# A graph layer with an expert mixture: six row buffers in the edge stage, two chunks of the first layer kept on chip

## The reference, cut to what matters

```python
# x [10000, 512]; src, dst [5000]; edge_attr [5000, 64]; dst is sorted
def gnn(x, edge_attr, edge_index, W_e, b_e, W1, b1, g1, beta1, W2, b2, g2, beta2, eps):
    src, dst = (edge_index[0], edge_index[1])
    msg = jax.nn.relu(x[src] + edge_attr @ W_e + b_e)
    aggr = jax.ops.segment_sum(msg, dst, num_segments=x.shape[0])
    h = (1.0 + eps) * x + aggr
    h = jax.nn.silu(_bn(h @ W1 + b1, g1, beta1))      # W1 [512, 1024]
    h = h @ W2 + b2                                   # W2 [1024, 512]
    return jax.nn.silu(_bn(h, g2, beta2))

x = x + gnn(_layernorm(x, axis=-1), ...)
x = x + ffn(_layernorm(x, axis=-1)[None], controller, f1, f2)[0]   # mixture of 16 experts
```

## Time and profile before

| | |
|---|---|
| median of 3 runs | 1946.03 (1945.61 to 1946.71) |
| profiled execution, its own time | 1943.54 |
| its span | 1941.8, mean granted clock 0.974 |
| TensorE busy | 1814.2, 93% |
| VectorE, ScalarE, GpSimd busy | 1184.6, 988.8, 364.1 |
| device memory | 171.31 MB read, 137.46 MB written |

### The profile page before, as it was taken

One profiled execution on the slowest core, in us unless ns is written; L12 is line 12 of the kernel. 1 busy time (PEld: TensorE's weight loads), 2 busy tenths in 40 slices (PEclk: granted clock), 3 DMA queues, 4 the chain that ended last, 5 costly groups with the idle time before them and its releaser, 6 DMA issues. The chain is left out here.

```text
span 1941.8 us, 40638 instructions
## 1 busy us (share of the span) xinstructions
PE 1814.2 (93%) x15580; PEld 1315.7 (68%) x15580; DVE 1184.6 (61%) x2341; ACT 988.8 (51%) x1716; POOL 364.1 (19%) x386
## 2 busy tenths in 40 slices
PE   5587699999999989999999987999999999999999
PEld 3354578888888878888888876565665665665654
DVE  6488466666666543333333336777778777777766
ACT  2355123333333356665566525667667667666653
POOL 4486320000000000000000014223222223222210
PEclk9777899999999999999999999999999999999999
DMA  9987756566566464433344237445455545455432
GB/s 366 304 170 109 172 170 169 169 169 169 169 177 181 141 264 146 163 136 127 129 159 155 84 112 235 135 141 161 134 144 156 145 140 158 135 152 158 126 89 86
DMA packets 209216, 310.81 MB, mean 160 GB/s; under 512 B 57234, under 2 KB 133970, under 8 KB 205875
## 3 DMA queue, kind: packets, MB, share of 16 engines
q1 hardware_dynamic: 200111, 287.84, 48.0%
q0 software_dynamic: 8960, 20.98, 5.6%
HBM read 171.31 MB, written 137.46 MB: 159 GB/s over the span
## 5 line engine op out<-in xcount | busy, mean ns | idle before, releaser
L1546 PE MATMUL bank<-f2s,inner_bd 128*32 128x512 f32 x2528 | 295.8, 596 | 0.6 <-DVE inner_bd L1149 0.5
L1445 ACT ACTIVATE inter_hi<-bank 128x512 fp32r<-128x512 f32 x316 | 189.2, 599 | 177.1 <-PE bank L1546 176.2
L599 ACT ACTIVATE h1o<-bank,b_by_channel 128x500 f32<-128x500 f32 x160 | 108.5, 678 | 324.6 <-PE bank L431 316.1
L1367 DVE TENSOR_TENSOR inter_lo<-bank,inter_hi 128x512 fp32r<-128x512 f32 x316 | 214.5, 688 | 57.6 <-ACT inter_hi L1445 53.1
L429 PE MATMUL bank<-hhi,w_hi 128*128 128x500 f32 x624 | 244.5, 392 | 0.0
L431 PE MATMUL bank<-hhi,w_lo 128*128 128x500 f32 x624 | 243.6, 390 | 0.0
L430 PE MATMUL bank<-hlo,w_hi 128*128 128x500 f32 x624 | 242.5, 389 | 0.0
L429 PE MATMUL bank<-ahi,w_hi 128*128 128x500 f32 x608 | 237.3, 390 | 0.0
L430 PE MATMUL bank<-alo,w_hi 128*128 128x500 f32 x608 | 236.6, 389 | 0.0
L431 PE MATMUL bank<-ahi,w_lo 128*128 128x500 f32 x608 | 236.4, 389 | 0.0
L563 DVE BATCH_NORM_STATS2 stats<-h1o 128x500 f32 (+1 forms) x160 | 103.2, 675 | 155.5 <-ACT h1o L599 155.5
(11 more groups left out here) (141 smaller groups left out, 3261.9 us busy)
## 6 DMA issues: line engine op xcount, KB each, us to landing
h1T<-h1o SPq DMA_DIRECT2D x19, 2000.0 KB, 8.1
h1in<-h1T SPq DMA_DIRECT2D x19, 2000.0 KB, 9.7
aggregate<-at SPq DMA_DIRECT2D x20, 1024.0 KB
x<-in_x SPq DMA_DIRECT2D x79, 256.0 KB, 2.9
x<-x SPq DMA_DIRECT2D x79, 256.0 KB, 3.6
x_back<-x SPq DMA_DIRECT2D x79, 256.0 KB, 3.0
out<-x_back SPq DMA_DIRECT2D x79, 256.0 KB, 2.2
h2in<-h2T SPq DMA_DIRECT2D x39, 512.0 KB, 4.1
```

Of the source, the lines that this page charges most:

```text
L599: nc.scalar.activation(h1o[b][:, m, :], mb[m % 4][:, 0:CW], ACT.Identity, bias=b1c[:, m:m + 1]).then_inc(evr, 1)
L1367: nc.vector.tensor_tensor(ilo[b][:, :], bI[b][:, :], ihi[b][:, :].bitcast(F32), ALU.subtract).then_inc(ilr, 1)
L1445: nc.scalar.activation(ihi[b][:, :], bI[b][:, :], ACT.Copy).then_inc(ihr, 1)
L1546: last = nc.tensor.matmul(bI[b][32 * i:32 * i + 32, :], ibd[:, e, j, :, :].rearrange("p s g -> p (s g)"), f2s[:, e, :], start=True, stop=True)
```

## The change

- **Row buffers.** Six windows of rows instead of four. Four lie in a tensor `rows_or_h1` that lives through both layers, the fifth and sixth in the memory of the first chunk of x and of `ht`. GpSimd gathers 24 tiles before it waits for the zeroing, takes four roots, and then three tiles behind the scatters of each window until all 40 are gathered; roots follow from window 1 on.
- **Zeroing** covers the 10000 rows only, 20 transfers instead of 21.
- **Loads tied to landings.** The vectors come first; x's first chunk waits for the landing of window 2 and the low parts of window 4, the four parts of W1 for the landings of windows 3, 4, 5 and 6.
- **Matches.** Comparison, mask and count are one instruction; the mask now includes the edge itself, and an edge goes to a spare row when its count is over 1.5.
- **Normalization** moves to ScalarE, as one activation with scale and bias behind `messages`; VectorE's first pass is then a plain add, relu is part of the rounding and of the low part. `bias(w + 1)` stands behind `combine(w)` on VectorE.
- **Clock keeping.** 8 calls behind the last window, 44 when the last but one has landed, 13 when the last has; none at the start of the first layer, 26 at its end, 8 instead of 20 at the start of the second. `add_up` waits for the previous window's evictions ahead of its wait for low parts.
- **Chunks on chip.** `h1o` is the first part of `rows_or_h1` and is kept by the second layer, which begins with chunks 18 and 19 from there, without store or load, and then takes chunks 0 to 17.

```diff
...
-XW = 4
+XW = 6
+GW = 3
...
-        xg = sb("xg", [P, XW * EW, H])
+        xg = first["rows"]
+        groups = [xg[:, w * EW:(w + 1) * EW, :] for w in range(XW - 2)] + [first["xt"][0], first["ht"]]
...
-        flat = agg.rearrange("a b -> (a b)").rearrange("(p c) -> p c", p=P)
+        flat = agg[0:N, :].rearrange("a b -> (a b)").rearrange("(p c) -> p c", p=P)
...
-                sp.dma_start(w1["whole"][:, :, :], W1.rearrange("(k p) n -> p k n", p=P)).then_inc(w1ld, 16)
                 with nc.allow_non_contiguous_dma(reason="vectors by channel"):
...
+                sp.wait_ge(sca, 16 * EW * 3)
+                sp.wait_ge(mlr, EW * (XW - 1))
...
+                for k in range(KH):
+                    sp.wait_ge(sca, 16 * EW * (k + 4))
+                    sp.dma_start(w1["whole"][:, k, :], W1[k * P:(k + 1) * P, :]).then_inc(w1ld, 16)
...
+                def normalize(w):
...
+                    for t in window(w):
+                        nc.scalar.activation(rows_of(t)[0:EP, :], rows_of(t)[0:EP, :], ACT.Identity, bias=nb[0:EP, t:t + 1],
+                                             scale=rs[0:EP, t:t + 1]).then_inc(nmr, 1)
...
-                        nc.scalar.activation(xg[0:EP, s, :], xg[0:EP, s, :], ACT.Relu, bias=nb[0:EP, t:t + 1]).then_inc(msr, 1)
...
-                        nc.scalar.activation(mhi[0:EP, t % (2 * EW), :], xg[0:EP, s, :], ACT.Copy).then_inc(mhr, 1)
+                        nc.scalar.activation(mhi[0:EP, t % (2 * EW), :], rows_of(t)[0:EP, :], ACT.Relu).then_inc(mhr, 1)
...
                 attributes(0)
+                normalize(0)
                 for w in range(EN):
...
                     if w + 1 < EN:
                         attributes(w + 1)
                     messages(w)
+                    if w + 1 < EN:
+                        normalize(w + 1)
...
-                nc.gpsimd.affine_select(out=before[:, :], in_=before[:, :], compare_op=ALU.is_gt, fill=0.0,
+                nc.gpsimd.affine_select(out=before[:, :], in_=before[:, :], compare_op=ALU.is_ge, fill=0.0,
...
-                def gather(w):
+                def gather(t):
+                    w = t // EW
                     if w >= XW:
...
-                    for t in window(w):
-                        nc.gpsimd.indirect_dma_start(
-                            out=xg[:, slot(t), :], out_offset=None, in_=x, in_offset=bass.IndirectOffsetOnAxis(
-                                ap=scol[:, t:t + 1], axis=0)).then_inc(gat[w % XW], 16)
+                    nc.gpsimd.indirect_dma_start(
+                        out=rows_of(t), out_offset=None, in_=x, in_offset=bass.IndirectOffsetOnAxis(
+                            ap=scol[:, t:t + 1], axis=0)).then_inc(gat[w % XW], 16)
...
-                for w in range(XW):
-                    gather(w)
-                for w in range(XW - 1):
+                for t in range(XW * EW):
+                    gather(t)
+                for w in range(4):
...
                 for w in range(EN):
                     scatter(w)
-                    if w + XW < EN:
-                        gather(w + XW)
-                    if w + XW - 1 < EN:
-                        root(w + XW - 1)
+                    for t in range(XW * EW + GW * w, min(XW * EW + GW * (w + 1), ET)):
+                        gather(t)
+                    if w >= 1 and w + 3 < EN:
+                        root(w + 3)
...
-                        nc.vector.tensor_scalar(sel[w % 3][i][0:EP, :], drow[0:EP, 0:(i + 1) * EP],
-                                                dcolf[0:EP, t:t + 1], None, ALU.is_equal).then_inc(sl, 1)
+                        nc.vector.scalar_tensor_tensor(
+                            out=sel[w % 3][i][0:EP, :], in0=drow[0:EP, 0:(i + 1) * EP], scalar=dcolf[0:EP, t:t + 1],
+                            in1=before[0:EP, (EW - 1 - i) * EP:EW * EP], op0=ALU.is_equal, op1=ALU.mult,
+                            accum_out=cnt[0:EP, t:t + 1]).then_inc(sl, 1)
...
-                    for t in window(w):
-                        i = t % EW
...
-                        nc.vector.tensor_tensor_reduce(out=scr[i][0:EP, :], in0=sel[w % 3][i][0:EP, :].bitcast(F32),
-                                                       in1=before[0:EP, (EW - 1 - i) * EP:EW * EP], scale=1.0, scalar=0.0,
-                                                       op0=ALU.mult, op1=ALU.max, accum_out=cnt[0:EP, t:t + 1]).then_inc(ct, 1)
...
-                def combine(w):
+                def bias(w):
...
+                def combine(w):
...
-                        nc.vector.scalar_tensor_tensor(out=xg[0:EP, slot(t), :], in0=xg[0:EP, slot(t), :],
-                                                       scalar=rs[0:EP, t:t + 1], in1=emb[t % EW][0:EP, :],
-                                                       op0=ALU.mult, op1=ALU.add).then_inc(prr, 1)
+                        dve.wait_ge(nmr, t + 1)
+                        nc.vector.tensor_tensor(rows_of(t)[0:EP, :], rows_of(t)[0:EP, :], emb[t % EW][0:EP, :], ALU.add)\
+                            .then_inc(prr, 1)
...
-                        nc.vector.tensor_tensor(mlo[0:EP, t % (2 * EW), :], xg[0:EP, slot(t), :],
-                                                mhi[0:EP, t % (2 * EW), :].bitcast(F32), ALU.subtract).then_inc(mlr, 1)
+                        nc.vector.scalar_tensor_tensor(out=mlo[0:EP, t % (2 * EW), :], in0=rows_of(t)[0:EP, :], scalar=0.0,
+                                                       in1=mhi[0:EP, t % (2 * EW), :].bitcast(F32), op0=ALU.max,
+                                                       op1=ALU.subtract).then_inc(mlr, 1)
...
+                bias(0)
...
+                bias(1)
                 for w in range(EN):
                     combine(w)
+                    if 2 <= w + 1 < EN:
+                        bias(w + 1)
                     if w + 2 < EN:
...
+                        pe.wait_ge(cbr, w * EW - 1)
...
                     add_up(w)
+                keep_clock(nc, tp, ident, 8)
+                pe.wait_ge(sca, 16 * (ET - EW))
+                keep_clock(nc, tp, ident, 44)
+                pe.wait_ge(sca, 16 * ET)
+                keep_clock(nc, tp, ident, 13)
...
-        h1o = [sb(f"h1o{i}", [P, KF, CW]) for i in range(2)]
...
-                keep_clock(nc, mb[3], ident, 16)
...
                 multiply(NCH - 1, 1, 0, KF)
+                keep_clock(nc, tb[0], ident, 26)
...
+                def columns(c):
...
+                    return span(c + NCH - 2 if static(c, 2) else c - 2)
...
                 def load(c, b):
-                    if not static(c, 2):
-                        sp.wait_ge(hir, (c - 1) * KF)
-                    sp.dma_start(h1[b][:, :, :], h1T[:, :, span(c)].rearrange("m p n -> p m n")).then_inc(ldh[b], 16)
+                    sp.wait_ge(hir, (c - 1) * KF)
+                    sp.dma_start(h1[b][:, :, :], h1T[:, :, columns(c)].rearrange("m p n -> p m n")).then_inc(ldh[b], 16)
...
-                for i in range(PIECES):
-                    ks = slice(i * KF // PIECES, (i + 1) * KF // PIECES)
-                    sp.dma_start(h1[0][:, ks, :], h1T[ks, :, span(0)].rearrange("m p n -> p m n")).then_inc(ldp[i], 16)
-                load(1, 1)
...
-                with sp.Fori(0, NCH // 2 - 1) as it:
+                load(2, 0)
+                store(0, 0)
+                load(3, 1)
+                store(1, 1)
+                with sp.Fori(1, NCH // 2 - 1) as it:
                     load(it * 2 + 2, 0)
                     store(it * 2, 0)
                     load(it * 2 + 3, 1)
                     store(it * 2 + 1, 1)
                 store(NCH - 2, 0)
...
-                        act.wait_ge(ldh[b], half(c, b, 16) - (16 if b == 0 else 0))
                     if not static(c, 2):
+                        act.wait_ge(ldh[b], half(c, b, 16) - 16)
...
-                        elif k % (KF // PIECES) == 0:
-                            act.wait_ge(ldp[k * PIECES // KF], 16)
...
-                        keep_clock(nc, psum[7], ident, 20)
+                        keep_clock(nc, psum[7], ident, 8)
...
+            rows_h1 = second.enter_context(nc.sbuf_tensor("rows_or_h1", [P, 4 * EW * H], F32))
+            h1 = [rows_h1[:, i * KF * CW:(i + 1) * KF * CW].rearrange("p (m n) -> p m n", m=KF) for i in range(2)]
...
+                chunk["rows"] = rows_h1[:, :].rearrange("p (t h) -> p t h", h=H)
...
```

54 lines of the change are left out of this document (21 added, 33 removed).

## The result

| | before | after |
|---|---|---|
| median | 1945.04 (6 runs, 1939.71 to 1946.71) | 1932.44 (6 runs, 1928.66 to 1934.27) |
| ratio to before, 95% interval | | 0.9941 [0.9929, 0.9953] |
| span of the profiled execution | 1941.8 | 1928.9 |
| mean granted clock | 0.974 | 0.987 |
| last landing | 207.65 | 198.72 |

12.6 faster by the medians (1932.44 against a forecast of 1934.3) and 12.9 by the spans. The shift vector is the last thing that VectorE works out from a layer's mean and variance; the next block's first activation needs it.

The account below looks back on a forecast made before the run. GpSimd's issue was taken to bind the edge stage's first windows, scatter plus landing the last. Edge −5.0, seam one −3.7 and seam two −3.0 make −11.7 from the median of 1946.03: 1934.3, range 1928 to 1941.

Parts of the forecast that it names:

- First scatter: Edge stage: less zeroing but eight more gathers ahead of its end move the first scatter by +2.5, to 75.7.
- Periods by GpSimd's issue: Edge stage, windows 1 to 4: three gathers instead of four shorten GpSimd's period from 14.04 to 12.7.
- idle time from window 5 on: Edge stage, listed as a sign: DMA idle of 1 to 3 per window from window 5.
- What transfers cost scatters: Edge stage: first landing 12.8; loads beside scatters add 0.8 for x, 0.3 and three times 0.6 for W1's pieces.
- everything hidden: Rival: loads beside scatters cost nothing; edge −8.5, seams −4.5 and −3.6, time 1929.4; chance 0.14.
- first rival: Edge stage: transfers cost in full, x and W1 competing with scatters; edge 0, seams −6.7, time 1939.3; chance 0.20.
- Arithmetic: Edge stage: VectorE at 10.3 and ScalarE's loop at 10.9 stay under the 12.7 period and cost nothing.
- slower rival: Edge stage: the loop through GpSimd, VectorE and ScalarE takes over; at 15 per window 1954.0; chance 0.08.
- Seam one: Edge stage to first layer: without 16 clock-keeping calls the first product comes earlier, −3.7.
- The clock: Seam one: −4.5 if TensorE's clock is up, −2.7 if it falls; −3.7 taken.
- lost case: Seam one with the clock fallen: 3.6 of products at half rate cost 1.8, leaving −2.7.
- Seam two: First to second layer: chunks 18 and 19 neither stored nor loaded, first product −3.0 (bounds −2.3 and −3.7).

Follow-up runs that it names:

- second comparison: Changed kernel and kernel before both run and profiled once more, unedited; changed 1935.18 against 1945.91 on the same chip, ratio 0.9947.
- W1 at once: Changed kernel, but W1 loaded whole in one transfer behind the zeroing, ahead of the vectors; ratio to before 0.9952.
- extra loads: Changed kernel plus two more loads of the same piece behind each of W1's four pieces, into memory nobody reads there; ratio to before 0.9959.
- old clock keeping: Changed kernel without the 65 calls at the edge stage's end, with 16 at the first layer's start again; 1939.61, ratio to before 0.9972.
- paired loads: Changed kernel with the aggregate's first chunk in four two-sub-tile loads instead of eight, 8 calls for 13, 23 for 26; 1936.21, ratio to before 0.9945.
- old arithmetic: Changed kernel with matches in two VectorE passes and ScalarE's scale and bias inside the messages as before; ratio to before 0.9947.

## Why the prediction was right, and where it was not

The total was within 1.9, and the gain is clear of its interval (10.7 in the second comparison, 1935.18 of 1945.91). The mechanisms are those of the text, but two sizes were off in opposite directions and one price was open: that the total came out this close is partly luck.

- **First scatter** +2.5: it came at 75.45 and 75.99, +2.3 and +2.6 against the two profiles of before. The two bounds were 0 and 5; the zeroing left out is −2.4 and the gathers +5.0, each in full.
- **Periods by GpSimd's issue**, 12.7 with three gathers and a root: 12.45, 12.94, 12.56, 12.79, and 13.95 to 14.17 with four. Right. The idle time from window 5 on, put at 1 to 3, was 2.4 to 5.7: four scatters alone take 7.5 of a period of 12, as the 5.02 of the earlier trace rows had shown. The gathers behind the scatters did not delay the landing: window 0 with three of them took 11.95 and window 5 with one 12.05, windows 6 and 8 without any 12.08 and 11.99.
- **What transfers cost scatters** is the term that was mis-sized. I had put 12.8 on the first landing, 0.8 on x, 0.3 and 3 × 0.6 on W1's pieces. Measured: first period 11.95 (−0.85), windows 1 to 4 50.7 for 51.9 (−1.2; x's 1.02 MB beside window 3 cost nothing that shows, 12.56), windows 5 to 7 37.1 for 38.4 (−1.3), the rest −0.4: 123.27 for 127.0. The landing moved by 8.9 where I had 5.0; the other profiles of the same edge stage give 7.2 to 8.1. That is the bound "everything hidden", which I held for the far end; the first landing of the earlier trace rows, 13.3 with 3 MB in flight, pointed the other way, but a piece is 0.52 MB and starts with a landed window. W1 at once (14.0 in window 0) and the extra loads (1.2 for 1.05 MB) show the price growing with the amount in flight. The first rival (0.20) had each scatter held up by the whole length of the transfer beside it; the runs show a price, and a half of that at most (1.2 for 1.05 MB, where 423 GB/s make 2.5).
- **Arithmetic** hidden: yes. The fused instruction takes 0.54 as priced, VectorE is busy 10.1 of 12.79 (10.3 forecast), and undoing the new arithmetic costs 0.3 to 2.2. The slower rival would have needed periods of 14.1 by this loop; none is there.
- **Seam one** −3.7: the first product moved by −3.96 (7.9 after the landing was forecast, and 8.2 to 8.5 is what the five profiles show that have the 65 calls and start the block as before). But it is not what the seam gave. The step that failed is that what comes behind the first product would come as it came. The 16 calls had covered two things. One is chunk 1's load of x, issued when the block starts: its statistics begin 11.1 to 13.2 after the last landing, and the five profiles at full clock then wait 0.3 to 1.7 for that chunk. The other is the clock: in the other six TensorE takes 12.5 to 13.2 to chunk 1's transposes, for 11.0 before, and five of these wait for nothing. Measured at the shift vector, the eleven profiles without the 16 calls average 490.2, the three with them 492.0: −1.8, or −2.5 where the clock held and −1.3 where it did not. I had asked after the third chunk's load at seam two, and not after the second's at seam one. One measurement stands against these marks: by the times the old clock keeping costs 4.4.
- **The clock** at that seam: the prediction took the middle between held (−4.5) and lost (−2.7). With no call the granted clock is 0.50 in the landing, with 65 (60 in the paired loads) it is 0.77 to 1.00. But the calls don't settle what it is behind the first product (1.00 in five profiles, 0.50 to 0.59 in five). The lost case had 1.8 for 3.6 of products at half rate, and no run shows that term as it stands. What the profiles show: before, the product of 0.79 ran at a granted clock of 0.50 and that of 0.39 at 1.00; in the second profile of the changed kernel three products take 1.25 at 0.50 (211.36 to 212.61) and 0.67 at 1.00 (213.74 to 214.41). In place of the 1.8, TensorE took 1.5 to 2.2 more up to chunk 1's transposes where the clock was 0.50 to 0.59, and the shift vector came 1.3 later on average.
- **Seam two** −3.0: −2.86 and −3.1 (3.71 for 6.57 and 6.83). The calls were to take 6.0 and the block to start as they end; they take 5.97 and it starts 0.3 later, and the run with 23 of them shows that they hold it (0.67 for three calls). Right.
- **The sum**: edge −8.9, seam one with its layer −3.6, seam two −2.9, mixture +2.5, in the profiles of the first comparison; −7.6, −1.0, −3.1 and +2.5 in the second (mixtures of 796.7 and 799.2). So the forecast of −11.7 was met partly by errors that cancel.
- **Open**: the mixture. Before it takes 794.5 and 796.7, in the twelve profiles that carry the change or most of it 794.6 to 802.7, 799.2 on average. The two profiles of the unchanged kernel differ by 2.2, and the paired loads reached 794.63 with the same mixture, so the length is not forced by the change; that it is on average 3.6 longer rests on two profiles of before. No experiment was made on it, but the rows show where a part arises. Before, and in the changed kernel:

```profile
1148.00 4.73 PE L1593 MATMUL bank<-ident 128*128 128x128 f32 x28 [4.57 <-PEq L742]
```

```profile
1132.59 6.24 PE L1605 MATMUL bank<-ident 128*128 128x128 f32 x28 [4.57 <-PEq L754]
```

These are the mixture's own calls of clock keeping, behind the same idle time. They take 4.7 to 4.9 in both profiles of before, in old arithmetic and in the paired loads (mixtures of 794.5 to 796.7), and 5.9 to 6.3 in the ten others (797.0 to 802.7); the granted clock in the 5 us behind the shift vector is 0.66 in the four and 0.50 in the ten. The first transposes behind them come 1.5 later in the changed kernel than before (1.3 in the second comparison), of the 2.5. The rest stays open.

## What to carry to other kernels

A queue that issues indirect transfers is a resource like an engine (here a gather takes 1.3 of it, and one gather more made a period 1.3 longer): count what stands between two of its binding instructions, and move one of them to where the queue waits anyway. Split a load into pieces that start when something has landed: here the first half megabyte beside a window was nearly free (0.2), 2 MB beside one cost 2.0. And when taking a delay out of a seam, ask what else became ready during it, a load or the clock; the first product alone does not tell what a seam gave. A mark further down the path (here the shift vector, 480 later) tells more, and the time has the last word where enough executions are there: for the old clock keeping they don't agree.

## What was not expected of the hardware

- Loads beside accumulating scatters cost more the larger they were, and not in proportion: 0.2 for 0.52 MB, 1.4 for 1.57 MB (both beside one of windows 4 to 7), 2.0 for 2 MB (beside window 0), where the zeroing's rate gives 1.2, 3.7 and 5.0. Each price rests on one profile of the kernel that sets it.
- A load of two sub-tiles in one transfer landed 4.06 after the last landing of the scatters, where one of a single sub-tile had landed by 3.87, although four issues take 1.67 and eight 3.27.
- TensorE was busy throughout the last landing (11.32 of 11.32) at a mean granted clock of 0.81 in the second profile of the changed kernel, and at 1.00 in the two kernels with old arithmetic (12.17 of 12.17 and 11.80 of 11.80), which have the same calls; the other profiles with them have 0.77 to 0.89.
- VectorE took 3.70 and 5.72 to normalize a chunk and add to it while GpSimd split the second half of W2, and 1.92 and 2.49 in the chunks before and after it. TensorE stood idle for 4.5 behind it in every profile. That the two engines hold each other up is not tested here.
